# A fused cross-attention and quantised FFN kernel: the first norm's scale and offset, one tap product and two low parts of x are placed or written otherwise

## The reference, cut to what matters

```python
x = x + xattn(layernorm(x), ctx, ctx, Wq, bq, Wk, bk, Wv, bv, Wo, bo)   # 16 heads, masked
x = x + ffn(layernorm(x), w1, conv_w, conv_b, w2)

def layernorm(x): return (x - mean(x)) / sqrt(var(x) + 1e-5)
def ffn(x, ...):                       # bit_linear: int8-rounded rows, ternary weights
    h = bit_linear(x, w1)              # 512 -> 2048 channels
    h = depthwise_conv1d(h, conv_w, conv_b)   # 3 taps over the rows, per channel
    return bit_linear(silu(h), w2)     # 2048 -> 512
```

## Time and profile before

| | |
|---|---|
| median of three executions | 1737.54 us |
| the profiled execution | 1740.04 us |
| its span, first to last instruction | 1738.3 us |
| TensorE busy | 1558.2 us (90%) |
| VectorE busy | 1433.3 us (82%) |
| ScalarE busy | 1028.6 us (59%) |
| GpSimd busy | 937.3 us (54%) |
| mean granted TensorE clock | 0.95 of full speed |

### The profile page before, as it was taken

How to read it: one execution, slowest core, us unless ns; L and a number is a source line. 1 busy time by engine, 2 the same in 40 slices (tenths; PEclk the granted TensorE clock), 3 DMA queues, 4 the chain that set the end, 5 groups by cost and what they waited for, 6 DMA issues and landing times.

```text
span 1738.3 us, 24605 instructions
## 1 busy us (share of the span) xinstructions
PE 1558.2 (90%) x9198; PEld 909.3 (52%) x9198; DVE 1433.3 (82%) x2217; ACT 1028.6 (59%) x1851; POOL 937.3 (54%) x774
## 2 busy tenths in 40 slices
PE   5978789799999999999999999999999999998875
PEld 3437446364646464555546464646555554646322
DVE  4485579789797979797988989797979798997887
ACT  3203138393948576675839393857667584939362
POOL 3000017475656484766747565757476675757453
PEclk9975879799999999999999999999999999999887
DMA  5551020202121030303130201103130303020000
GB/s 151 161 141 34 0 62 1 61 1 62 33 42 60 1 86 1 86 1 90 19 86 1 61 26 35 52 5 85 19 86 1 86 1 86 1 62 1 27 20 31
DMA packets 77558, 80.99 MB, mean 47 GB/s; under 512 B 29248, under 2 KB 55104, under 8 KB 76927
## 3 DMA queue, kind: packets, MB, share of 16 engines
q1 hardware_dynamic: 77439, 79.43, 16.9%
HBM read 34.55 MB, written 19.42 MB: 31 GB/s over the span
## 4 chain that ended last, share of the span: by engine, by line
DVE 38%; issue 22%; PE 16%; ACT 12%; POOL 10%; DMA 1%; SPq 0%; DVEq 0%; ACTq 0%; POOLq 0%
DVE negm L1505 9%; DVE h L1420 8%; POOL h L573 5%; ACT hqb L1022 5%; DVE gall L1345 5%; ACT pexp L1064 4%; POOL gall L571 4%; PE ps L598 3%; DVE qhl L1466 2%; PE ps L742 2%; PE ps L748 2%; DVE hl L1462 2%; DVE xr L1552 1%; PE ps L918 1%; DVE nw L1304 1%
## 5 line engine op out<-in xcount | busy, mean ns | idle before, releaser
L571 POOL TENSOR_TENSOR gall<-gall,cw 128x512 f32<-128x512 f32 x235 | 251.3, 1069 | 257.8 <-DVE h L1420 257.8
L573 POOL TENSOR_TENSOR h<-h,gall 128x512 f32<-128x512 f32 x235 | 329.9, 1404 | 18.4
L576 POOL TENSOR_TENSOR h<-h,r 128x512 f32<-128x512 f32 x240 | 306.4, 1324 | 43.9 <-DVE qb L1545 28.1
L1420 DVE SCALAR_TENSOR_TENSOR h<-gall,cw,h 128x512 f32<-128x512 f32 x256 | 258.6, 1015 | 63.6 <-ACT h L1083 63.6
L742 PEld LDWEIGHTS ps<-va,pexp 128*128 128x128 f32 x2048 | 268.4, 197 | 30.0 <-issue 10.9
L748 PE MATMUL ps<-xqT,w1T 128*128 128x512 f16 x1024 | 260.7, 383 | 17.9 <-DVE gall L1345 17.2
L1345 DVE SCALAR_TENSOR_TENSOR gall<-ps,bias,srow 128x512 f32<-128x512 f32 x256 | 190.1, 743 | 103.9 <-PE ps L748 79.1
L742 PE MATMUL ps<-va,pexp 128*128 128x33 f32 x2048 | 265.6, 275 | 0.0
L918 PE MATMUL ps<-w2T,hqb 128*128 128x512 fp8e4 x960 | 242.5, 381 | 0.0
L1022 ACT ACTIVATE hqb<-h 128x512 f16<-128x512 f32 x256 | 156.0, 669 | 126.0 <-PE ps L918 120.6
L1083 ACT ACTIVATE h<-gall,cb,cw 128x512 f32<-128x512 f32 x256 | 221.7, 866 | 8.5
(11 more groups left out here) (216 smaller groups left out, 2359.4 us busy)
## 6 DMA issues: line engine op xcount, KB each, us to landing
qs<-qhl SPq DMA_DIRECT2D x192, 128.0 KB, 2.6
xr<-in_x SPq DMA_DIRECT2D x16, 1024.0 KB, 5.6
out<-xr SPq DMA_DIRECT2D x64, 256.0 KB
h<-in_L_ffn_w SPq DMA_DIRECT2D x8, 1024.0 KB, 8.4
kst<-kh_scratch SPq DMA_DIRECT2D x32, 38.5 KB
h<-in_L_xattn_Wk SPq DMA_DIRECT2D x1, 1024.0 KB, 5.7
xr<-in_ctx SPq DMA_DIRECT2D x1, 1024.0 KB
h<-in_L_xattn_Wv SPq DMA_DIRECT2D x1, 1024.0 KB, 10.6
```

What stands on the lines that cost most here:

```text
L571: gp.tensor_tensor(right, right, cw[:, c, 2:3].to_broadcast([P, TB]), ALU.mult).then_inc(c2m_ok, 1)
L573: gp.tensor_tensor(hc(c), hc(c), right, ALU.add).then_inc(c2p_ok, 1)
L576: gp.tensor_tensor(hc(c), hc(c), r2[:], ALU.mult).then_inc(u_ok, 1)
L1420: ve.scalar_tensor_tensor(out=hc(c), in0=g[:, c % 4, 1:TB + 1], scalar=cw[:, c, 1:2], in1=hc(c), op0=ALU.mult, op1=ALU.add).then_inc(c1_ok, 1)
```

## The change

Three edits. (1) GpSimd does the whole of the first norm's scale and offset: from the variance it makes `var + EPS`, the power, the Newton step (written with the sign turned), the offset and the scale, eight operations, each but the last waiting for the one before; `pw1` now counts 8 a slot and `ln1` 2. VectorE keeps the statistics only, and ScalarE waits for `pw1`. (2) GpSimd's tap product is a `tensor_scalar` with the weight as one scalar per partition, in place of a `tensor_tensor` with the weight broadcast over 512 columns. (3) The low parts 0 and 1 of x are issued in step 13 ahead of the dequantisation of tile 13, parts 2 and 3 stay behind the tap of tile 11.

```diff
@@ gpsimd, slot
+                def norm1():
+                    def step(k):
+                        pool.wait_ge(pw1, at(s, 8, 8 + k))
+                    var, y0, y1, neg = (nw1[:, k, :] for k in range(4))
+                    pool.wait_ge(ln1, at(s, 2, 4))
+                    if do_a:
+                        pool.wait_ge(xn_ok, at(s, TT, TT))
+                    gp.tensor_scalar(var, mv1[:, :, 1], EPS, None, ALU.add).then_inc(pw1, 1)
+                    step(1)
+                    gp.tensor_tensor(y0, var, mhalf[:], ALU.pow).then_inc(pw1, 1)
+                    step(2)
+                    gp.tensor_tensor(y1, y0, y0, ALU.mult).then_inc(pw1, 1)
+                    step(3)
+                    gp.tensor_tensor(y1, y1, var, ALU.mult).then_inc(pw1, 1)
+                    step(4)
+                    gp.tensor_scalar(neg, y1, 0.5, -1.5, ALU.mult, ALU.add).then_inc(pw1, 1)
+                    step(5)
+                    gp.tensor_tensor(neg, neg, y0, ALU.mult).then_inc(pw1, 1)
+                    step(6)
+                    gp.tensor_tensor(nb1[:], mv1[:, :, 0], neg, ALU.mult).then_inc(pw1, 1)
+                    gp.tensor_scalar(y1, neg, -1.0, None, ALU.mult).then_inc(pw1, 1)
                 for c in range(CT):
                     if do_q and c == 5:
-                        pool.wait_ge(ln1, at(s, 7, 10))
-                        gp.tensor_tensor(nw1[:, 1, :], nw1[:, 0, :], mhalf[:], ALU.pow).then_inc(pw1, 1)
+                        norm1()
...
-                        gp.tensor_tensor(right, right, cw[:, c, 2:3].to_broadcast([P, TB]), ALU.mult).then_inc(c2m_ok, 1)
+                        gp.tensor_scalar(right, right, cw[:, c, 2:3], None, ALU.mult).then_inc(c2m_ok, 1)
@@ scalar, normalise1
-                        act.wait_ge(ln1, at(s, 7, 14))
+                        act.wait_ge(pw1, at(s, 8, 16))
@@ vector
                 def norm1_stats():
-                    dve.wait_ge(ln1, at(s, 7, 8))
+                    dve.wait_ge(ln1, at(s, 2, 3))
+                    if do_a:
+                        dve.wait_ge(pw1, at(s, 8, 8))
...
-                    dve.wait_ge(ln1, at(s, 7, 9))
-                    ve.tensor_scalar(nw1[:, 0, :], mv1[:, :, 1], EPS, None, ALU.add).then_inc(ln1, 1)
-
-                def norm1():
-                    dve.wait_ge(pw1, at(s, 1, 2))
-                    rsqrt(ln1, s, 7, 10, nw1)
-                    if do_a:
-                        dve.wait_ge(xn_ok, at(s, TT, TT))
-                    ve.scalar_tensor_tensor(out=nb1[:], in0=mv1[:, :, 0], scalar=-1.0, in1=nw1[:, 2, :],
-                                            op0=ALU.mult, op1=ALU.mult).then_inc(ln1, 1)
@@ vector, the loop over c
+                    if do_q and c == 13:
+                        x_low(0)
+                        x_low(1)
                     if do_f:
                         if c < CT:
                             dequant(c)
...
-                    if do_q and c == 8:
-                        norm1()
                     if do_q and c == 13:
-                        for k in range(KT):
-                            x_low(k)
+                        x_low(2)
+                        x_low(3)
```

## The result

The changed kernel takes 1813.03 us (median of 4 runs, 1812.18 to 1813.68) against 1739.16 (4 runs, 1737.44 to 1743.97): a ratio of 1.042 [1.040, 1.044], 74 us slower. The forecast was 1727 us, with 1716 to 1745 around it. The profiled execution took 1813.68 us with a span of 1811.9, and a mean granted clock of TensorE of 0.925 (before 0.950).

What follows compares the result with a forecast made beforehand. ScalarE's wait for tile 9's dequantisation, ahead of a gapless stretch, was taken as the bound. Ten slots at 0.9 us plus 1.7 us in the last gave 10.7 us: 1740.04 to 1729.3 profiled, 1727 as median, range 1716 to 1745.

Steps and rivals of the forecast that it cites:

- The product: GpSimd's third-tap product as tensor_scalar: 0.63 us instead of 1.04 undisturbed, also saving 1.7 us in the last slot with taps.
- nearer row (one streamed input): GpSimd select timings, 0.29 us at 128 columns and 0.45 at 308, extended at 0.9 ns a column to price the product.
- GpSimd's small chain becomes the bound: Rival, between tiles 4 and 5 on GpSimd: the eight norm operations delay tile 9; 1753, up to near 1800; chance 0.17.
- my low end of 3.4: Norm's chain on GpSimd: seven small operations at 0.33 us plus 1.1 us for pow, 3.4 us; high end 9.4.
- a block that did not come: Norm's chain on GpSimd: 0.7 us added for mutual holding-up with VectorE's two-operand SBUF operations, making 4.1 us.
- shrinks with three cheaper products, and must do so: GpSimd's tail, where ScalarE waited 0.82 us for tile 15: it must shrink for the earlier tile 9 to shorten the slot.
- ScalarE's wait before tile 9: ScalarE idles 1.14 us for tile 9's dequantisation; the change recovers 0.9 us a slot in ten slots, 9.0 us.
- 10.7 us: The forecast's total gain: 9.0 us from ten steady slots and 1.7 us from the last slot with taps.
- those slots gain nothing: The three slots that begin a batch, and the first steady one: masks make TensorE later in the former; no gain.
- No gain: Rival: product stays at 1.04 us, norm takes 4.1, tile 9's dequantisation ends at 840.1, nothing moves; 1737; chance 0.17.
- The order of the low parts: Two low parts fill VectorE's 1.20 us idle time before tile 13; a stall there was counted within "no gain".
- TensorE's wait for the low parts of x: TensorE's 1.33 us wait: projection begins 2 us earlier, of which only the 0.9 us shift counts.

Runs made afterwards that it cites:

- E5: The changed kernel with the constant 0.5 in place of the per-partition weight in GpSimd's tap product: 1800.4 us, ratio 1.0361.
- E3: The kernel before with only GpSimd's tap product made a tensor_scalar with one scalar per partition: 1788.36 us, ratio 1.0286.
- E1: The changed kernel with the tap product as before (tensor_tensor, weight broadcast); norm on GpSimd and early low parts stay: 1736.41 us, ratio 0.9995.
- E9: The changed kernel with 16 unused 240-column matrix products per steady slot on TensorE ahead of tile 11's product: 1804.35 us, ratio 1.0377.
- E6: E1 with the broadcast tap product on only 256 of the 512 columns: 1731.33 us, ratio 0.9958.
- E4: The kernel before with only low parts 0 and 1 of x issued ahead of tile 13's dequantisation: 1746.56 us, ratio 1.0051.
- E2: E1 with all four low parts behind tile 13's tap as before, so only the norm moves to GpSimd: 1751.48 us, ratio 1.0072.
- E8: E1 with tile 5's third tap on VectorE and tile 7's on GpSimd in exchange: 1732.27 us, ratio 0.9959.
- E10: E8 with the four low parts of x in their old place: 1732.6 us, ratio 0.9968.
- E11: The changed kernel with all four low parts behind tile 13's tap (norm and product, without the order): 1810.78 us, ratio 1.0416.
- E12: The changed kernel with the tensor_scalar tap product on only 256 of the 512 columns: 1734.67 us, ratio 0.9981.
- E7: E1 with tile 5's third tap also on VectorE, beside tile 7's: 1736.49 us, ratio 0.9985.

## Why the prediction was wrong

**The product.** This step failed, and it carries the whole result. I took 0.63 us from the slope of two selects, 0.9 ns a column, as the "nearer row (one streamed input)", and my other ends were no gain (1.04) and 1.30, the price of a full addition. It is 1.57 undisturbed, outside all three. A one-input operation seemed bounded from above by a two-input one of the same size, and it was not: E5 shows that the form costs, not the scalar's address. Against the old product it adds 0.53 us in each of 15 tiles, 8 us a slot; GpSimd's idle time takes in a good half of that, and some 3.6 us a slot (E3's 51 us over 14 slots, the half clock in it counted) come through; 2.8 where no half clock touches the slot.

The Trainium skill, GPSIMD Engine Reference, section 4.1, says that one-input work on GpSimd runs at roughly line rate and two-input work about twice as slow as on VectorE. The runs contradict the first half for this operation: 1.57 us with one streamed input, against 1.04 for the same product with a broadcast operand and 1.30 for the two-input addition. The second half fits: that 1.30 stands against 0.69 us for VectorE's 128x512 operation with two inputs in SBUF (L1434 of the kernel before).

**Where the price fell.** The rival "GpSimd's small chain becomes the bound" had the place right (tile 9's dequantisation waits 4.55 us for GpSimd, and TensorE stalls behind it) and the cause wrong. Its chain is 2.9 us, below even my low end of 3.4: an operation on 4 columns is 0.20 us and the gap to the next 0.08, where I had 0.33 for both and added a block that did not come. What made tile 9 late are the dear products of the tiles up to 4, which start the norm 0.87 us later in the slot than in E1 (862.78 - 818.67 against 830.01 - 786.77), and that of tile 5 behind it, 0.53: together 1.40, and tile 9 is 1.39 later than in E1. And no case of mine had the end of the slot, where 2.7 us are lost: I had written that the tail "shrinks with three cheaper products, and must do so"; with dearer ones it grew, and E3 shows it as the larger part.

**The clock.** No step looked at what a longer wait on TensorE sets off. 0.98 us of idle time before tile 11's product left the clock at 2.4 GHz; 1.70 us was followed by some 10 us at 1.2 GHz in most slots. E9 shows 8.7 us of the 74 that come from it, net of what the filling costs; what the 30.7 us at half clock that E9 keeps are worth, no run shows.

**ScalarE's wait before tile 9.** This mechanism was right. With the price that I had assumed (E6) the wait of 1.14 us vanishes and the slot shrinks by 1.23, where I had 0.9. Yet E6 gains 7 us, not 10.7. The step that misses there is "those slots gain nothing" for the slots that begin a batch: they lose 1.0 to 1.8 us each, 4.4 together, by the tap of tile 15 and some half clock.

**"No gain".** With the product at 1.04 (E1) this rival is what happens, 1736.41, but for another reason than its own. It had the norm at 4.1 us and tile 9 unmoved; in fact tile 9 comes 0.67 us earlier, and half of that goes again before the maxima, 0.12 of it in tile 15's tap itself (0.87 us), the batch slots losing 1 us each (taps of 1.68 to 1.78).

**The order of the low parts.** I cost it at nothing. Alone it is 9 us slower (E4), the norm alone 14 us slower (E2), both together even (E1), and at the end it makes no difference (E8 and E10, E11 and the change). The parts do not add up; I take it that each shifts where VectorE's taps meet GpSimd's additions. The one meeting that I could tie to the slot's length is the tap of tile 15: against 0.75 free it takes 1.25 in E10, 1.38 in E4, 1.39 in E12 and 1.59 in E7, and the stretch from tile 9 to the maxima grows by 0.5, 0.7, 0.7 and 0.9, with 23.9 behind it in all of them. For E2 that is not the whole: this tap takes 1.52 and the stretch is 1.0 longer, and what the half clock in five of its slots comes from is open. So is the half clock in E3.

The Trainium skill, SBUF — State Buffer, "Who interferes with whom", says that a VectorE operation with two SBUF inputs and a GpSimd one that reads SBUF exclude each other. For GpSimd's additions and small operations the traces agree (taps of 1.38 to 1.68, additions of 1.6, small ones of 0.56 to 0.70). For the one-input product they agree in one direction only. The tap at 869.35 lies wholly inside the product from 868.63 to 870.20, and neither is longer than when alone (0.74 and 1.57); of the 160 taps that start during a product of the changed kernel none takes more than 0.77 us. But the 16 products that start while a tap runs take 2.00 us (2.01 at 888.93).

TensorE's wait for the low parts of x, at least, fell with the new order as I had said, from 19.9 us to 7.5 in the changed kernel, and was worth nothing, as I had said too:

```profile
L622 PE MATMUL ps<-hl,WqT 128*128 128x512 f16 x768 | 173.2, 383 | 7.5 <-DVE hl L1478 7.5
```

## What to carry to other kernels

Price an operation by a row of the same operation, engine and shape; where there is none, another kind's row is no safe bound, above or below (two selects gave 0.63 us here, a two-input addition 1.30, and the product took 1.57), and one short run of the operation alone is worth more than the rest of the sum. A step that makes an engine wait a little longer may cost more than its wait: look whether TensorE's stall grows, and read the granted clock behind it. When an engine's work is moved by less than a microsecond, look at the last operation ahead of the long gapless stretch, for that is where a collision with the other engine's reads is paid in full.

## What the runs showed of the hardware

- GpSimd, float32, 128x512: multiplication by a scalar per partition 1.57 us, by a constant 1.49, by a broadcast operand 1.04, addition of two full operands 1.30. At 256 columns 0.92 for the scalar form and 0.61 for the broadcast one. All of these undisturbed.
- GpSimd, 128x4: multiplication or addition 0.20 us, with a wait on the one before 0.08 more; pow 1.04.
- GpSimd's product by a scalar and a VectorE tap with two inputs in SBUF: a product that starts while a tap runs takes 2.00 us instead of 1.57 (16 cases), a tap that starts during a product is not held up (160 cases).
- TensorE in a stream that is otherwise dense: ten times it stood idle for 1.68 to 1.73 us before tile 11's product. Seven times the granted clock then fell to 1.2 GHz for some 10 us, once for 6.8 us (from 1466.4, 1.3 us after the product had started), twice (at 869.49, after 1.69 us, and at 1562.50) it stayed at 2.4 GHz.
